# The key projection moved behind the query projection in TensorE's order of one step

## The reference

```python
h = table[x]                                  # 32 x 128 x 256
h = h + attention(layernorm(h))               # 16 heads of 16, causal softmax, output projection
xf = layernorm(h);  logits = xf @ wg          # 8 experts, the best one for each token
rank = cumsum(one_hot(top1)) - 1              # place within the expert; beyond the capacity: no expert
h = h + gather(gelu(slots @ W1 + b1) @ W2 + b2) * score_of_top1
```

## Time and profile before

| | us |
|---|---|
| median of three timed runs | 590.61 (589.71 to 597.28) |
| the profiled execution, its own time | 588.22 |
| its span (first to last instruction) | 586.5 |
| TensorE matmul busy | 545.4 (93%) |
| VectorE busy | 442.6 (75%) |
| ScalarE busy | 327.6 (56%) |
| GpSimd busy | 260.3 (44%) |

### The profile page before, as it was taken

How to read it: one execution, slowest core, us unless ns; L and a number is a source line. 1 busy time by engine, 2 the same in 40 slices (tenths; PEclk the granted TensorE clock), 3 DMA queues, 4 the chain that set the end, 5 groups by cost and what they waited for, 6 DMA issues and landing times.

```text
span 586.5 us, 14243 instructions
## 1 busy us (share of the span) xinstructions
PE 545.4 (93%) x5179; PEld 465.0 (79%) x5179; DVE 442.6 (75%) x1196; ACT 327.6 (56%) x728; POOL 260.3 (44%) x346
## 2 busy tenths in 40 slices
PE   6876899999999999998889799999999999999991
PEld 4655777777888887876554699999999999999991
DVE  7435689999999999988646495969687787959550
ACT  3413666566666666665523583839293938475620
POOL 6635777778677667765653003030303030212111
PEclk9988999999999999999879999999999999999996
DMA  3799887777778777672112403333343425130000
GB/s 111 191 267 292 262 264 231 232 244 242 236 214 231 237 233 206 202 239 83 39 64 73 154 9 123 113 109 127 106 131 99 136 73 161 36 129 16 22 21 13
DMA packets 45109, 87.52 MB, mean 149 GB/s; under 512 B 7219, under 2 KB 34090, under 8 KB 41392
## 3 DMA queue, kind: packets, MB, share of 16 engines
q1 hardware_dynamic: 39024, 73.82, 41.5%
q0 software_dynamic: 5248, 12.66, 6.6%
q10 hardware_dynamic: 768, 0.13, 0.1%
HBM read 53.63 MB, written 31.69 MB: 145 GB/s over the span
## 4 chain that ended last, share of the span: by engine, by line
PE 75%; DVE 10%; DMA 6%; issue 3%; POOL 2%; ACT 1%; SPq 0%; POOLq 0%; ACTq 0%
PE M L688 13%; PE PV L1299 12%; PE S L1280 10%; PE C L1280 10%; PE M L1299 8%; PE PV L834 6%; PE S L727 5%; PE C L740 4%; PE M L630 3%; DVE mx L920 2%; PE M L709 2%; PE M L1245 2%; DMA ks<-k_parts 1%; DMA k_parts<-kp 1%; DMA q_parts<-qp 1%
## 5 line engine op out<-in xcount | busy, mean ns | idle before, releaser
L1172 POOL DMA_INDIRECT out_dram<-ys,xs x40 | 39.7, 993 | 209.2 <-DVE ys L1352 194.2
L535 ACT ACTIVATE pt<-C 128x512 f32<-128x512 f32 x128 | 76.3, 597 | 66.0 <-PE C L740 65.3
L477 POOL TENSOR_SCALAR_AFFINE_SELECT pt<-pt 128x512 f32<-128x512 f32 x128 | 81.1, 641 | 42.3 <-ACT pt L535 41.5
L920 DVE TENSOR_REDUCE mx<-S 128x4 f32<-128x512 f32 x128 | 86.4, 681 | 9.1 <-PE S L727 8.8
L1380 DVE TENSOR_TENSOR hl<-gl,hh 128x258 fp32r<-128x258 f32 (+1 forms) x128 | 62.7, 492 | 34.5 <-ACT hh L1213 31.6
L1220 ACT ACTIVATE gl<-S,biases 128x384 f32<-128x384 f32 (+1 forms) x64 | 34.0, 533 | 54.9 <-PE S L1280 54.0
L1213 ACT ACTIVATE hh<-gl 128x258 fp32r<-128x258 f32 (+1 forms) x128 | 59.4, 471 | 0.0
L834 PE MATMUL PV<-pt,va 128*32 128x128 f32 x1024 | 55.0, 288 | 3.0 <-issue 1.3
L727 PE MATMUL S<-ks,qs 128*128 128x128 bf16 x512 | 51.2, 225 | 7.0 <-DMA ks<-k_parts 3.0
L1299 PE MATMUL PV<-weh,hh 128*128 128x256 f32 x192 | 55.1, 287 | 0.0
L727 PEld LDWEIGHTS S<-ks,qs 128*128 128x128 bf16 x512 | 29.8, 99 | 31.4 <-issue 23.6
(11 more groups left out here) (180 smaller groups left out, 1657.7 us busy)
## 6 DMA issues: line engine op xcount, KB each, us to landing
w_raw<-in_L_ffn_W_dram SPq DMA_DIRECT2D x32, 512.0 KB, 6.4
qs<-q_parts SPq DMA_DIRECT2D x48, 256.0 KB
ks<-k_parts SPq DMA_DIRECT2D x48, 256.0 KB
q_parts<-qp SPq DMA_DIRECT2D x16, 384.0 KB, 2.6
k_parts<-kp SPq DMA_DIRECT2D x16, 384.0 KB
rows_of_slots<-w_raw SPq DMA_DIRECT2D x6, 877.5 KB, 8.5
xs<-rows_of_slots SPq DMA_DIRECT2D x7, 650.0 KB
out_dram<-h SPq DMA_DIRECT2D x16, 256.0 KB, 6.6
```

Of the source, the lines that this page charges most:

```text
L477: pool.affine_select(out=buf[:, :, :], in_=buf[:, :, :], compare_op=ALU.is_ge, fill=0.0, base=0, pattern=[[0, 4], [1, S]], channel_multipl ...
L535: act.activation(pt[u % 4][:, :, :], bC[u % 2][:, :].rearrange("p (j t) -> p j t", j=4), ACT.Exp, scale=SCALE).then_inc(a_exp, 1)
L920: dve.tensor_reduce(mx[g.slot][:, 4 * (u % QUADS):4 * (u % QUADS) + 4, u // QUADS], bS[u % 2][:, :].rearrange("p (j t) -> p j t", j=4), AX ...
```

## The change

In the unit with `s == 1` TensorE now issues, behind `S` and `C`, the ranks' products of group `i-5`, the query projection of group `i`, the key projection of group `i`, and then `PV`. In the unit with `s == 2` only the transposes of `os` stand between `C` and `PV`. All waits stay with the instructions that they belonged to; no other engine's program changes.

```diff
                     g = group(n, i)
-                    if g and s == 2:
-                        wait(pe, a_nm, g.back(3).times(1, 1))
-                        wait(pe, v_base, g.back(5).times(1, 2))
-                        wait(pe, a_V[1], g.times(1))
-                        project(g, bM2, 1).then_inc(pe_K, 1)
                     if g and s == 7:
...
-                    g = group(n, i)
-                    if g and s == 1:
-                        wait(pe, a_xth, g.times(1, 1))
-                        wait(pe, v_xtl, g.times(1, 1))
-                        project(g, bM0, 0).then_inc(pe_Q, 1)
                     g = group(n, i - 5)
                     if g and s == 1:
...
                                   ).then_inc(pe_rk, 1)
+                    g = group(n, i)
+                    if g and s == 1:
+                        wait(pe, a_xth, g.times(1, 1))
+                        wait(pe, v_xtl, g.times(1, 1))
+                        project(g, bM0, 0).then_inc(pe_Q, 1)
+                    g = group(n, i)
+                    if g and s == 1:
+                        wait(pe, a_nm, g.back(3).times(1, 1))
+                        wait(pe, v_base, g.back(5).times(1, 2))
+                        wait(pe, a_V[1], g.times(1))
+                        project(g, bM2, 1).then_inc(pe_K, 1)
```

## The result

| | before | after |
|---|---|---|
| median of the timed runs, us | 590.64 (4 runs) | 601.64 (4 runs, 600.23 to 602.05) |
| ratio, 95% interval | | 1.0161 [1.0127, 1.0194] |
| profiled execution, its own time, us | 588.22 | 602.05 |
| its span, us | 586.5 | 600.3 |

The changed kernel is 1.6% slower, between 1.3 and 1.9%. (The plain quotient of the two medians is 1.0186, inside the same interval.) The forecast was 598, a ratio of 1.013.

A forecast was written before the change was run, and what follows sets the result against it. TensorE was taken as the bound, busy 15.67 of 15.70 us. Steps 9 to 15 +5.95, step 8 +0.5, steps 5 to 7 -0.7, step 4 +0.6, step 3 +1.1: together +7.5 us, so 598 on the median's scale; range 588 to 605.

The forecast's parts named there:

- the chain over ScalarE: Exponential of unit 2, second query part, first key part, `kr`, maxima of unit 3: delays the maxima's transpose by 0.46 us.
- step 8: Step after the burst steps, with a smaller surplus than theirs: set at +0.5 us.
- the step itself: Each full step, 9 to 15: 0.85 us longer, bounds 0.2 and 1.5; 5.95 us over seven steps.
- steps 5 to 7: Steps with GpSimd's burst: surplus of 1.09 us goes and 0.85 comes, -0.24 each, -0.7 in the sum.
- the last term: End of VectorE's chain in a step: about 0.12 us later, making the ranks' wait 0.27 in later steps.
- won back ahead of the output projection: Between the maxima's transpose and the output projection: some 0.20 us regained, 1.21 now against 1.01 without a wait.
- The four waits: TensorE in a step: ranks on `oh` 0.15, keys on `base` 0.13, `on`'s transposes 0.04, maxima's transpose 0.46 us.
- The ranks' wait for `oh`: Ranks, now ahead of the query projection, wait for VectorE's `oh`: 0.15 us, in later steps 0.27.
- rival A: VectorE becomes the bound, its operations perhaps colliding with GpSimd's: 1.5 us a step, 605; above 603, chance 0.16.
- Steps 3 and 4: Early steps: step 3 +1.1 us by a later maxima's transpose, step 4 +0.6; step 2 absorbs its lateness.
- B: Rival, faster: burst lateness gone from steps 5 to 8, no wait of the maxima's transpose; 587, below 588, chance 0.09.
- C: Rival, nothing: waits short, some 0.2 us a step; 589.5, between 588 and 592.5, chance 0.15.

The follow-up runs named there:

- run 4: Changed kernel with, on ScalarE, the keys' first part ahead of the exponential of unit 2 and the second query part; 595.48 us, ratio 1.0039 to the kernel before.
- run 1: The changed kernel again, unaltered, for a second profile; 602.62 us (one run).
- run 2: Kernel before with the ranks' products alone moved ahead of the query projection, key projection still in unit 2; 596.62 us, ratio 1.0068.
- run 3: Changed kernel with the ranks' products back behind the query projection and ahead of the key projection; 607.11 us, ratio 1.0203 to the kernel before.
- run 6: Changed kernel with matmuls on constants filling TensorE's early waits, 18 in step 2 and 5 in step 3; 602.72 us, ratio 1.0161 to the kernel before.
- run 9: Kernel before with the changed order in steps 5 to 15 alone, steps 0 to 4 as before; 598.30 us, ratio 1.0135.
- run 10: Kernel before with the changed order in steps 0 to 4 alone, steps 5 to 15 as before; 593.22 us, ratio 1.0005.
- run 11: Kernel before with the ranks' products ahead of the query projection in steps 5 to 7 alone; 588.44 us, ratio 0.9946.
- run 7: Kernel before with the ranks' products ahead of the query projection and, on VectorE, `route` ahead of `xtl`; keys in unit 2; 593.94 us, ratio 1.0005.

## Why the prediction was right, and where not

**Direction and mechanism.** Right. TensorE had nothing to win from an earlier key projection in the later steps, and lost by new waits. Run 4 shows the chain over ScalarE at work: taken out, it gives back 0.24 us a step. That the total came near is in part luck: the terms erred by +0.8 (step 8) and +2.4 (the long `oh`) on one side and by -1.0 (the step itself) and -0.4 (steps 5 to 7) on the other.

**The places in a step.** Each came within 0.06 us of the forecast (keys, `PV`, `on`, the transpose, the output projection). The step itself got 0.71 us longer instead of 0.85: the last term, 0.12 for VectorE's lateness at `oh`, did not arise where `oh` was short. Wait by wait, from the distances between starts and against step 10 of before: ranks 0.17 us (forecast 0.15), keys 0.13 (0.13), `on` 0.06 (0.04), maxima 0.36 (0.46); 0.21 is won back ahead of the output projection (0.20). The four waits make 0.72, and the step got 0.71 longer. What offsets the 0.21 won back is mostly the 0.16 by which the transposes of `os` are dearer ahead of `PV` (0.53) than ahead of the keys (0.37); the prediction set such differences at nothing, but its walk had this one in it, since its four waits make 0.78 and its start came 0.93 later. A signal took 0.05 to 0.06 us as assumed, though the row named for it gives 0.03. The profile shows only 0.20 us of idle time ahead of the transpose of the maxima, where I had announced 0.46: the `C` ahead of it has a recorded length of 0.39, of which 0.22 is the usual distance to the next start, so that 0.58 between the starts appears as 0.20 of idle time and is 0.36 of lateness. The start times carry the reading, not the idle times.

**The ranks' wait for `oh`.** This is the term that was mis-sized. I took 0.15 to 0.27 us. It is 0.7 to 1.0 in steps in which `oh` meets GpSimd's select of unit 0, which starts 0.13 to 0.15 us behind it in nearly all of steps 9 to 15 with VectorE's order unchanged. Over ten such profiles (before, after, and runs 1 to 4, 6 and 9 to 11) that is so in 68 of 70 steps, and `oh` took 0.82 or 0.83 in 34 of the 68 and 0.17 in all the others but one (0.31). In the kernel before it was 0.17 in seven of seven, so that these steps didn't show the risk; the earlier trace rows showed it at another place, `pm`, and I used it only for steps 5 to 8 and for rival A. The trace before did hold it for `oh` itself, in step 17, which I had not looked at:

```profile
275.67 0.69 DVE L1018 TENSOR_TENSOR oh<-iota,first 128x16 bf16<-128x16 f32 x1
...
276.42 0.18 PE L811 MATMUL M<-oh,trib 128*128 128x8 bf16 x1 [0.80 <-DVE oh L1018]
```

The Trainium skill ("SBUF — State Buffer", section "Who interferes with whom") says that an operation of VectorE with two inputs in SBUF contends with one of GpSimd that reads SBUF, calls the ports that they share an exclusive lock, and says that the order of issue decides which one blocks. Each long `oh` in steps 9 to 15 agrees: it ends 0.03 or 0.04 us behind the select, which keeps its 0.65 us.

Three long ones in a profile are 2.4 us. For steps 5 to 15 the forecast was 5.75; the profiles differ by 7.6, and run 9 measured 1.35% of 592, 8.0 us (interval 3.9 to 12.1, which holds the forecast too).

**Step 8.** This term was mis-sized as well: +1.3 us instead of +0.5. The ranks, now first in the queue, wait 0.85 us for an `oh` that comes late by itself, which the query projection had hidden; all profiles with the ranks ahead of the queries there and VectorE's order as before have 16.8 to 17.5 us in it. Part of it may be time won in steps 5 to 7 and given back, as in run 11, where step 8 is long with the queries first; the runs don't separate the two.

**Steps 5 to 7.** The burst's lateness left as said: 16.35 to 16.46 instead of 16.74 (-1.1 us in all, forecast -0.7), and `on` no longer waits. Run 2 shows that the ranks' move gives this. The kernel with that move in these steps alone, run 11, is 0.5% faster, but its rows show that step 8 takes more than half of the gain back.

**Steps 3 and 4.** The wait in step 3 is 1.20 us, as worked out (some 1.1 more). Whether its price on the total is the 1.7 us of the sum is not shown: run 10 puts it at 0.3 us with an interval of -1.8 to +2.4, which holds both that and nothing. In the profile of run 10, without a late fall of the clock, steps 3 and 4 are 1.1 us longer than before; in that of the changed kernel, with one, 5.7. That step 2 would absorb the earlier lateness held: its transpose comes at 49.10 instead of 48.76 us.

**The rivals.** B and C are out: the waits arose. A, VectorE as the bound, is out in a step with a short `oh`, since run 4 shortens it with VectorE's work unchanged; its second half, that operations of VectorE collide with GpSimd's, is what steps 13 to 15 show.

**What stays open.** Why the clock is granted low in some executions as late as 54 to 62 or 66 to 74 us. Nearly every profile has such a stretch between 38 and 54 us, that of the kernel before too; a second, later one stands in those of the changed kernel, but also in run 7 (0.60 from 66 to 70 us) and in the fastest, run 11 (0.57), so that it isn't tied to the order of the projections alone. The wait of 5.46 us for the keys in step 2 stands in several orders as well (5.07 in run 11). What decides whether `oh` or the select goes first, and a change of GpSimd's order that keeps them apart, weren't tried. What makes up the 0.47 us a step that run 4 keeps over the kernel before (`oh`, `base`, `on`, the transposes ahead of `PV`) was read off the starts, and not taken out piece by piece. Why `oh` comes late in step 8 is followed back one link only: `xtl` ahead of it had waited 0.45 us for `xth` of ScalarE.

## What to carry to other kernels

A projection that stands in an engine's order between two dependent pieces of work is cover: before it is moved, look up what the other engines do under it, and walk the chain of the new neighbours link by link through each hand-written queue; here such a walk gave every start of a step with a short `oh` to within 0.06 us. A small operation of VectorE that the bound engine waits for should not be left to start beside one of GpSimd, even if one trace shows it short every time; 1.5 us of other work ahead of the waiter made the same 0.65 us of delay cost almost nothing. And a move that loses as a whole may win in the steps in which it meets a burst, but then the next step must be looked at too.

## What the runs showed of the hardware

In steps 9 to 15 `oh`, 16 elements on each of 128 partitions, took either 0.17 or 0.82 us (once 0.31) with a GpSimd select of 0.65 us recorded as starting 0.14 us later. The likely reading is that the short ones got in ahead of the select and the long ones did not; the recorded start doesn't tell which, as it is the same in both. Within one execution one outcome can prevail (seven of seven long in run 11, none in the kernel before), and it differs between two executions of the same kernel (steps 13 to 15 in the first, 10, 13 and 14 in run 1). A select is not needed for a long one: in step 17 of all 13 profiles `oh` took 0.69 or 0.70 us without overlapping a select, and ended within 0.04 us of the end of GpSimd's indirect DMA operation of 1.04 us (`DMA_INDIRECT` in the profile). In step 16 it started at the same distance from such an operation and took 0.17. The cause of that difference is open.
